# A row-wise normalized linear layer in 8 cores: fourteen pairs of output blocks for twelve, the first of them made plainly beside the last tiles' arrival

## The reference

```
x = L0_attn_x                                    # (1, 8192, 4096), float32
xn = layernorm(x)                                # over the last axis, eps 1e-5
# "attention" over a leading axis of length 1: the softmax is over one score, so its message is xn
x = x + (xn + xn)
h = layernorm(x)
y = x + einsum('bsi,oi->bso', h, aa * tanh(kk * weight)) + bias     # weight (4096, 4096)
```

## Time and profile before

| | us |
|---|---|
| time, median of 3 runs (lowest, highest) | 471.12 (470.56, 473.22) |
| time of the profiled execution | 471.84 |
| its span, slowest core (1) | 470.3 |
| spans of the 8 cores | 462.9 to 470.3 |
| TensorE busy | 434.6 (92%) |
| VectorE busy | 320.8 (68%) |
| GpSimd busy | 203.8 (43%) |
| ScalarE busy | 193.8 (41%) |

### The profile page before, as it was taken

The page is one execution under the profiler, slowest core; times in us unless marked ns, Lnnn a source line. Parts: engine busy times, 40 slices in busy tenths (PEclk is TensorE's granted clock), DMA queues, the critical chain, the costliest instruction groups (busy, mean ns, idle before and its releaser), DMA issues.

```text
span 470.3 us, 7035 instructions; the slowest of 8 cores (462.9 to 470.3 us)
## 1 busy us (share of the span) xinstructions
PE 434.6 (92%) x2184; PEld 206.2 (44%) x2184; DVE 320.8 (68%) x474; ACT 193.8 (41%) x181; POOL 203.8 (43%) x188
## 2 busy tenths in 40 slices
PE   0656789999999999989999999999999999999997
PEld 0634345544444444434444444444444444444443
DVE  2788687487642899999675858675656666667552
ACT  0478767637933414124424243424333333333000
POOL 0222112122530861397637464647473838386300
PEclk9857998999999999999999999999999999999999
DMA  7999999974999759659997959795959696957101
GB/s 172 313 288 319 302 348 298 288 224 147 295 276 315 263 195 293 211 156 289 302 325 231 343 166 312 235 305 195 324 180 325 201 319 212 329 168 284 57 31 60
DMA packets 36612, 116.37 MB, mean 247 GB/s; under 512 B 5088, under 2 KB 5088, under 8 KB 36576
## 3 DMA queue, kind: packets, MB, share of 16 engines
q1 hardware_dynamic: 23472, 84.43, 56.6%
q0 software_dynamic: 5760, 18.88, 14.0%
q10 hardware_dynamic: 7344, 12.62, 7.2%
HBM read 99.14 MB, written 16.78 MB: 246 GB/s over the span
## 4 chain that ended last, share of the span: by engine, by line
PE 64%; DMA 16%; DVE 6%; DVEq 5%; ACT 3%; issue 3%; SPq 2%; ACTq 0%
PE acc L755 55%; DMA wr<-wpieces 12%; PE acc L735 7%; DMA early<-x 4%; DVEq L479 3%; PE acc L706 2%; SPq L289 1%; ACT late L618 1%; DVEq L520 1%; DVEq L532 1%; ACT early L626 1%; DVE early L524 1%; DVE late L503 1%; DVE h2T L503 1%; SPq L295 0%
## 5 line engine op out<-in xcount | busy, mean ns | idle before, releaser
L676 ACT ACTIVATE late<-wr,kk_sb 128x1024 bf16<-128x1024 f32 x48 | 53.3, 1143 | 96.1 <-PE acc L755 41.8
L676 ACT ACTIVATE early<-wr,kk_sb 128x1024 bf16<-128x1024 f32 x48 | 53.4, 1143 | 87.6 <-PE acc L755 44.6
L755 PE MATMUL acc<-h2T,late 128*128 128x512 bf16 x384 | 85.0, 379 | 1.4 <-DVE late L524 1.4
L755 PE MATMUL acc<-h2T,early 128*128 128x512 bf16 x384 | 84.8, 379 | 0.0
L735 PE MATMUL acc<-early,h2T 128*128 128x512 bf16 x256 | 62.4, 395 | 3.3 <-ACT early L618 3.3
L755 PEld LDWEIGHTS acc<-h2T,late 128*128 128x128 bf16 x384 | 37.5, 98 | 47.0 <-issue 1.8
L755 PEld LDWEIGHTS acc<-h2T,early 128*128 128x128 bf16 x384 | 37.6, 98 | 45.3
L735 PE MATMUL acc<-late,h2T 128*128 128x512 bf16 x256 | 57.0, 379 | 0.0
L537 DVE SCALAR_TENSOR_TENSOR early<-acc,early 128x512 f32<-128x512 f32 x48 | 33.2, 692 | 33.0 <-PE acc L755 26.8
L537 DVE SCALAR_TENSOR_TENSOR late<-acc,late 128x512 f32<-128x512 f32 x48 | 33.2, 692 | 31.9 <-PE acc L755 28.8
L368 POOL TENSOR_TENSOR early<-early 128x512 f32<-128x512 f32 x24 | 34.6, 1440 | 40.4 <-DMA early<-xt 29.5
(11 more groups left out here) (58 smaller groups left out, 428.4 us busy)
## 6 DMA issues: line engine op xcount, KB each, us to landing
wr<-wpieces SPq DMA_DIRECT2D x128, 512.0 KB, 7.9
early<-x SPq DMA_DIRECT2D x24, 512.0 KB, 13.8
early<-xt POOLq DMA_DIRECT2D x24, 256.0 KB, 6.9
late<-xt POOLq DMA_DIRECT2D x24, 256.0 KB, 6.3
yt<-early ACTq DMA_DIRECT2D x24, 256.0 KB, 5.0
yt<-late ACTq DMA_DIRECT2D x24, 256.0 KB, 6.3
h2T<-x SPq DMA_DIRECT2D x8, 512.0 KB, 19.9
y<-late POOLq DMA_DIRECT2D x16, 256.0 KB, 7.0
```

The lines of the kernel that those rows point to most:

```text
L676: scalar.activation(slot[b, j % 2][:, k * PW:(k + 1) * PW], wr[w % RING][:, :], AF.Tanh, bias=0.0, scale=kk[:, :]).then_inc(s_wt, 1)
L755: mm = tensor.matmul(acc[pbank[j, m]][:, :], slot[b, j % 2][:, k * 128:(k + 1) * 128], a[:, :, k * 128:(k + 1) * 128], start=(k == 0), sto ...
```

## The change

- NO is 1: only 512 outputs are made token-major, and there are NP = 14 pairs. The second token-major group with its loads of x, its part of the bias and its evictions is gone.
- Pair 0 is made plainly, as 4 groups (token half i, output block o) of 32 matmuls: units `("G", i, o, p)`, 8 matmuls with W piece p of the pair. Groups of token half 0 stand around the transposes of tiles 6 and 7 in place of `second`, those of half 1 behind tile 7's products, and then the 13 other pairs begin. VectorE takes each of its four results with one instruction (`take_first`).
- `ARRIVAL` has four pieces, not three, between the x of tiles 6 and 7, so that piece 20 stands ahead of tile 7. `TANH_BEFORE` is 21 and 24 for tiles 6 and 7, not 20 and 26.
- The sum for M5 is made ahead of the evictions before tile 6's statistics. The other sums of h and the W sums of pair 1 stand behind `spread()`, those for M2, M7 and M1 first.
- GpSimd's bases for pairs 0 and 1 follow one another and wait for `s_sa` >= 4, the first four sums of h; pair 1's loads wait for the stores of tiles 4 to 7.
- W blocks of even pairs lie in `late`, those of odd pairs in `early`, where group 0's W was: ScalarE waits for all eight token-major groups before it makes those of pair 1. The sums and the rows have other places too.

```diff
-NO = 2
+NO = 1
 ARRIVAL = [...
-           ("x", 4), ("w", 3), ("x", 5), ("w", 4), ("x", 6), ("w", 3), ("x", 7), ("b", 1)]
-
-TANH_BEFORE = [1, 4, 7, 10, 13, 16, 20, 26]
+           ("x", 4), ("w", 3), ("x", 5), ("w", 4), ("x", 6), ("w", 4), ("x", 7)]
+
+TANH_BEFORE = [1, 4, 7, 10, 13, 16, 21, 24]
...
     products(5)
-    for p in range(3):
-        todo += second(p)
-    join(6, [], second(3))
+    todo += [("G", 0, 1, 0), ("G", 0, 1, 1), ("G", 0, 1, 2)]
+    todo += [("T", 6, 0), ("T", 6, 1), ("G", 0, 1, 3), ("T", 6, 2), ("G", 0, 0, 4), ("T", 6, 3)]
     products(6)
-    for p in range(4, 6):
-        todo += second(p)
-    join(7, [], second(6))
+    todo += [("G", 0, 0, 5)]
+    todo += [("T", 7, 0), ("T", 7, 1), ("G", 0, 0, 6), ("T", 7, 2), ("G", 0, 0, 7), ("T", 7, 3)]
     products(7)
...
+    todo.insert(len(todo) - 6, ("R", 0))
+    todo += [("G", 1, 1, 0), ("R", 1), ("G", 1, 1, 1), ("G", 1, 1, 2), ("G", 1, 1, 3)]
+    todo += [("G", 1, 0, p) for p in range(4, 8)]
     return todo
...
+    sA5, sA2, sA1 = part(late, 0, 16), part(early, 0, 16), part(early, 56, 16)
...
+        slot[n, 0], slot[n, 1] = part(late, 16 + 4 * i, 4), part(early, (40, 44, 48, 52, 16, 20)[i], 4)
...
+    pool = [(6, ("rc", 4)), (7, ("rc", 4))] + sorted(free, key=lambda v: v[1][0] != "ev")
+    order_of = [FIRST] + [PRODUCTS] * (NP - 2) + [LAST_PRODUCTS]
...
@@ GpSimd
             elif j == 1:
-                for t in range(4):
+                for t in range(4, NT):
                     gpsimd.wait_ge(s_y[t], 16 * NO)
...
+        for q in QUARTERS:
+            load_xt(1, q)
+        gpsimd.wait_ge(s_rc, 4)
+
+        gpsimd.wait_ge(s_sa, 4)
+        for j in range(2):
+            for q in QUARTERS:
+                residual(j, q)
...
@@ VectorE
             if t == 6:
+                wait_transposed(vector, 3, NCH - 1)
+                add_tiles(tiles(sA5), quarter(0, 0), quarter(0, 1), ALU.add)
                 for i in range(5):
                     evict(i)
...
         spread()
+        evict(6)
+
+        for c in range(NCH):
+            wait_normalized(vector, 6, c)
+        wait_transposed(vector, 7, NCH - 1)
+        add_tiles(tiles(sA2), quarter(1, 0), quarter(1, 1), ALU.add)
+        vector.wait_ge(s_mm, nth_product[0, (0, 0)])
+        add_tiles(quarter(0, 1), quarter(0, 1), quarter(1, 1), ALU.subtract)
         evict(7)
...
+        add_tiles(tiles(sA1), quarter(0, 0), quarter(1, 1), ALU.add)
+        sums(1, ["S6", "D12"])
+        sums(1, ["S7", "D21"])
+        vector.wait_ge(s_mm, nth_product[0, (1, 0)])
+        add_tiles(quarter(1, 0), quarter(1, 0), quarter(0, 0), ALU.subtract)
+        sums(1, ["S1"])
         vector.wait_ge(s_bc, 16)
...
+        for q in FIRST:
+            take_first(q)
+        for j in range(1, NP):
             vector.wait_ge(s_bs[0, 1], j + 1)
             vector.wait_ge(s_bs[0, 0], j + 1)
             take(j, "M5", [(0, 1, 1, False), (0, 0, -1, False)])
-            sums(j, ["S1"])
+            if j > 1:
+                sums(j, ["S1"])
...
@@ ScalarE
-        while w < W0:
+        while w < W0 + 8:
             tanh_piece(w)
             w += 1
         copy_rows(0)
...
+        scalar.wait_ge(s_grp, NT)
+        for j in range(1, NP + 1):
+            if 2 <= j < NP:
+                scalar.wait_ge(s_mm, made(j - 2))
...
+                if b == "B12" and j == 2:
+                    for i, q in enumerate(FIRST):
+                        store(0, q, i + 1)
```

More of the change, by code:

```diff
@@ L191, in build_nc @@
     s_base = sem("s_base")
-    s_b0 = [sem(f"s_b0{i}") for i in range(2)]
+    s_b0 = sem("s_b0")
     s_nD = sem("s_nD")
@@ L482, in evict, with add_tiles @@
                                         ALU.add, ALU.add).then_inc(s_ev, 1)
+        def add_tiles(out, a, b, op):
+            for i in range(4):
+                vector.tensor_tensor(out[:, i, :], a[:, i, :], b[:, i, :], op)
+            vector.drain().then_inc(s_sa, 1)
         vector.memset(ones[:, :], 1.0)
@@ L512, in sums @@
                     vector.wait_ge(s_wt, W0 + 8 * j + 8)
-                if n == "S7" and j == 1:
-                    for t in range(4, 6):
+                if n == "S6" and j == 1:
+                    vector.wait_ge(s_row, 4)
+                if n == "S6" and j == 2:
+                    for t in range(4):
                         vector.wait_ge(s_y[t], 16 * NO)
-                if n in ("S6", "S7") and j >= 2:
-                    vector.wait_ge(s_mm, len(PRODUCTS) * (j - 1))
+                if n in ("S6", "S7") and j >= 3:
+                    vector.wait_ge(s_mm, made(j - 2))
+                if n == "S1":
+                    vector.wait_ge(s_mm, nth_product[j, "M5"])
                 if n in ("D12", "D21", "S1"):
@@ L613, in tanh_piece @@
         def tanh_piece(w):
[L614 to L616 removed]
             scalar.wait_ge(s_w[w % RING], 16 * (w // RING + 1))
[L618 to L619 removed]
+            if w < W0:
+                out = wp[:, w * PW:(w + 1) * PW]
+            else:
+                j, b, k = (w - W0) // 8, BLOCKS[(w - W0) // 2 % 4], w % 2
+                out = slot[b, j % 2][:, k * PW:(k + 1) * PW]
+            scalar.activation(out, wr[w % RING][:, :], AF.Tanh, bias=0.0, scale=kk[:, :]).then_inc(s_wt, 1)
         def normalize(t):
@@ L654, in copy_rows, with store @@
                 scalar.copy((srow, brow)[half][:, 512 * i:512 * (i + 1)], acc[6 + i][:, :]).then_inc(s_rc, 1)
-        while w < W0:
+        def store(j, q, read):
+            scalar.wait_ge(s_rd, reads(j) + read)
+            r = 256 * j + 128 * q[1]
+            scalar.dma_start(yt_h[r:r + 128, 512 * q[0]:512 * (q[0] + 1)], C(j, q)).then_inc(s_so[j % 2, q], 16)
+        while w < W0 + 8:
             tanh_piece(w)
@@ L723, in _ @@
                 continue
+            if u[0] == "G":
+                _, i, o, p = u
+                if W0 + p >= seen_w:
+                    seen_w = W0 + p + 1
+                    tensor.wait_ge(s_wt, seen_w)
+                wait_transposed(tensor, 4 * i + 3, NCH - 1)
+                if p % 4 == 0:
+                    kind, n = bank_free["G", i, o]
+                    tensor.wait_ge({"ev": s_ev, "rd": s_rd}[kind], n)
+                b = BLOCKS[p // 2]
+                a = quarter(i, int(b[1]) - 1)
+                for k in range(8 * (p % 2), 8 * (p % 2) + 8):
+                    mm = tensor.matmul(acc[bank_of["G", i, o]][:, :], slot[b, 0][:, k * 128:(k + 1) * 128],
+                                       a[:, :, k * 128:(k + 1) * 128],
+                                       start=(p % 4 == 0 and k == 0), stop=(p % 4 == 3 and k == 15))
+                if p % 4 == 3:
+                    mm.then_inc(s_mm, 1)
+                continue
             _, t, ot, p = u
@@ L740, in _ @@
                 mm.then_inc(s_grp, 1)
-        for j in range(NP):
+        for j in range(1, NP):
             for m in order_of[j]:
@@ L745, in _ @@
                 b, what, nb = B_OF[m]
-                if na and j == 0:
+                if na and j == 1:
                     tensor.wait_ge(s_sa, na)
```

173 lines of the change are left out of this document (50 added, 123 removed).

## The result

The changed kernel takes 475.92 us (median of 16 runs) where the kernel before takes 471.39 in the same number. The ratio is 1.0099, 95% interval 1.0078 to 1.0121; like all ratios here it leaves out executions in which the cores of one die ran at a lower granted clock and took longer. The changed kernel is slower by 1%. The forecast was 472.2 us in a range of 467.0 to 477.0, with no measurable change as the likeliest outcome and slower at 0.33.

The account below looks back on a forecast made before the run. TensorE was taken as the bound: after 71 us, its number of matmuls plus waits. Terms -4.8 + 5.7 + 0.3 = +1.2 us on 470.3 gave 471.5 of span, forecast 472.2 us, range 467.0 to 477.0.

Parts of the forecast that it names:

- Removed work, and the waits that go: TensorE: 16 matmuls fewer, 3.46 us off; waits of 1.93 us in the pairs and 1.01 at tile 7 go.
- Tile 6: Before tile 6's transposes TensorE waits 1.45 instead of 0.15 us, +1.30; the sum for M5 adds 0.3, bounds 0 and 1.
- The clock at tile 6: No half-clock cost was counted behind the wait at tile 6; pair 1 was to start at 147.2.
- Tile 7's x behind a W piece: Tile 7's x goes ten microseconds later, behind W piece 20; cost 0, its statistics starting at 104.23.
- the fourth rival: Tile 7's x comes late behind the W piece; 3 us of lateness give 475; chance 0.07.
- The bases: GpSimd's bases of pairs 0 and 1 run 29.2 us, from 144.3 to 173.5, drawn out beside seven VectorE sums.
- The rule of an exclusive port: VectorE and GpSimd lock each other out; each of seven sums costs GpSimd up to 1.16 us, the end 1.3 later.
- Waits in pairs 1 and 2: TensorE stalls 5.7 us in all at M6 of pair 1 and M3, M4 of pair 2; D21 at 184.0.
- The round of residuals in pair 2: Pair 2's base (0,0) at 193.8, D21 of pair 3 at about 208; no more cost, but no room.
- the rival in which it costs: Pair 2's residual round trip decides: loads of 8.2 us put base (0,0) near 200; 477 to 478; chance 0.15.
- The clock in the pairs: Slower clock after M4's part of the stall, about 2.5 us: 0 to 1.3 us, taken as 0.3.

Follow-up runs that it names:

- Filling the gap: Changed kernel with pair 0's fourth unit ahead of tile 6's transposes, not among them; ratio to the kernel before 1.0101 in the second series.
- Mending GpSimd's order alone: Changed kernel with all four loads of pair 2's residuals issued together, not two behind a base; ratio to the kernel before 1.0023.
- the two runs with early sums: Changed kernel with pair 2's S6 and D12 right behind pair 0's takes, then also ScalarE's third W block ahead of the stores; ratios 1.0172 and 1.0153.
- small bases: Changed kernel with GpSimd computing only 8 of 512 columns of each base for pairs 0 and 1; ratio to the kernel before 1.0000.

## Why the prediction was right, and where it was off

The direction of the whole was right: TensorE's work falls by 3.5 us, and what VectorE and GpSimd must have ready some 26 us earlier takes it back. The time lay in the range, 3.7 us above the forecast. But the outcome that I held likeliest did not come: the loss of 4.5 us is more than the 2.4 that I called no change, and it lies outside my own 469 to 474, where I had given slower 0.33. Of the 3.7 us, 1.3 lie between span and time: the median is 2.0 us over the profiled span, and I took 0.8. The other 2.4 are in the sum, 473.9 for 471.5 of span: +0.3 for the wait at tile 6, +1.7 for the half clock behind it, +1.3 for pair 3, -0.5 for the waits in pairs 1 and 2, -0.3 for the clock there. By its steps:

- *Removed work, and the waits that go*: right. 16 instructions fewer, no wait at tile 7.
- *Tile 6*: the wait of 1.45 us with 0 to 1 for the sum for M5 became 2.01. The sum took 5.46 us instead of 4.62 and held up the first eviction, which came at 88.41 instead of 87.98: 0.43 us, for 0.3 taken. TensorE was also through 0.14 us sooner than worked out.
- *The clock at tile 6*: missed. I had the half clock on record for long waits and priced it only for M4. Behind the 2.01 us at tile 6 it cost 1.69 us, on three cores of eight. Pair 1 started at 148.74 and not at 147.2. Filling the gap took wait and half clock away and changed the time by nothing that can be told, so most of this went into the forecast of the start and not into the end.
- *Tile 7's x behind a W piece*: right, no cost. Its statistics at 104.68 run 4.84 us without a pause; the fourth rival falls.
- *The bases*: right in mechanism, off in size both ways. The start was 147.8 instead of 144.3, my upper bound: the eviction ended at 137.3 instead of 135.8, the store took 7.3 instead of 5.6 us from the start of its issue, and the four issues 2.6 instead of 2.2. The length was 27.3 instead of 29.2, since an instruction alone takes 1.32 us from start to start over a pair, not 1.4, and a blocked one 0.87 more. Seven were drawn out, the number forecast. They ended at 175.1 for 173.5. The rule of an exclusive port (the Trainium skill, page "SBUF — State Buffer", section "SBUF: two separate sides") agrees with these rows: every one of the seven loses about the rest of a VectorE sum, and with no overlap none does.
- *Waits in pairs 1 and 2*: forecast 5.7 us in all, measured 5.16; D21 of pair 2 releases M4 at 185.5 for 184.0. Part of this closeness is luck: D21 came 1.5 us late, and TensorE began pair 1 late by as much, for the unpriced half clock, so that the two errors cancel. M6 shows it too. Its bank was free at 164.26, for 164.2 forecast, but TensorE wanted it at 162.7 and not at 161.0, and the wait was 1.54 and not 3.2. The sums of pair 1 waited 2.30 and 1.79 us for ScalarE's W; VectorE took up S7 at 148.5 for 147.2, and TensorE did not wait for it.
- *The round of residuals in pair 2*: this is the step that failed. I wrote "no more cost, but no room" and gave the rival in which it costs 0.15, to decide from about 195 for base (0,0). That base was ready at 195.1 and not at 193.8, and D21 of pair 3 at 211.1, where TensorE wanted it at 210.0. It cost 1.33 us on the profiled core. Mending GpSimd's order alone took 0.0076 off the ratio, 3.6 us and some three quarters of the whole loss of 4.5; the two runs with early sums lost more for its sake. The first chain, the late bases, and this second one lie in series: shortening only the first moved the wait to the second (small bases), and vice versa some 5 us of waits stayed in pairs 1 and 2.
- *The clock in the pairs*: I took 0.3 us, with 1.3 as a bound. On the profiled core nothing; on five of the other seven a group of 16 matmuls behind a wait of 2.2 to 3.3 us took 5.30 instead of 3.61, 1.7 us.

What stays open: whether the load of (0,0) takes 4.8 or 8.3 us because W pieces stand ahead of it was read from the order of issues over the cores and not tried by itself. Whether filling the gap at tile 6 gains up to 2 us is not settled either.

## What to carry to other kernels

When a cheaper form of a stage lets the bound engine arrive earlier, list what the others must have ready by then, in their queue order, before counting the saving; here a form with 3.5 us of matmuls less brought the need forward by some 26 us. When one late chain is found, look for the next in series: taking a base's cost away moved the wait to the loads behind it. And issue loads when their place is free, not when the loop comes to them: that one reordering of four transfers was worth 0.0076, as much as the whole removal of 16 matmuls (3.5 us of 471).

## What the runs showed of the hardware

- The length of a wait alone does not say whether half clock follows. Behind 2.01 us at tile 6 TensorE ran 8 matmuls in 3.58 us instead of 1.89, at 1.2 GHz (clock 0.66 on average from 104 to 109 us); behind waits of 2.01 to 2.10 us at the same place four other cores did not slow down, nor did the same core behind 2.32 us at M4 of pair 2. Over the timelines of all eight cores, of the changed kernel and the experiments, I counted 109 waits of 2.2 us or more ahead of the pairs' matmuls. Of the 41 under 3.2 us, 18 had a slowed group behind them (5.1 to 6.5 us for 16 matmuls instead of 3.61, or 8.8 for 32 instead of 7.07); of the 68 longer ones, up to 6.6 us, all had (5.0 to 6.6 us for 16, 8.7 to 10.0 for 32), which is 1.3 us and more on top of the wait. The division at 3.2 us is mine, and one wait of 2.06 us, below the count, had a slowed group behind it too.
- A GpSimd instruction on two SBUF operands (128x512, f32) takes 1.27 us alone and 2.06 to 2.25 when a VectorE sum of two bf16 operands is in its way. One of only 8 columns is held up as well: those of the small bases took 0.20 us, and 0.99 to 1.18 beside the adds for M6. VectorE's takes from PSUM took 0.69 to 0.75 us in both cases.
- The same 256 KB load took 3.6 to 5.8 us from issue to use over the eight cores in one order of the queues, and 6.7 to 8.9 on ten cores of two other runs where four W pieces were asked for more than 2 us ahead of it.
